# Attention scores laid out head by head, block transposes of the probabilities on VectorE, softmax shift and residual on GpSimd

## The reference

```python
# per sequence; z = layernorm of x + a projection of attention-pooled block sums
qkv = z @ W_attn + b_attn                       # heads: H = 32, D = 8, S = 32 tokens
scores = einsum('bhqd,bhkd->bhqk', q, k) / sqrt(8)
scores = where(causal, scores, -10000) + alibi  # cols <= rows
probs = softmax(scores, axis=-1)
x = x + (einsum('bhqk,bhkd->bhqd', probs, v) merged) @ W_proj + b_proj
hs = GRU(cond, x)                               # 32 dependent steps
x = x + hs @ (weight * scale).T + bias
```

## Time and profile before

| | |
|---|---|
| median of three runs | 445.61 us |
| the profiled execution | 445.15 us, of which the span is 443.3 us |
| attention stage, with the start | the first 257 us of the span |
| GRU stage | the rest |
| PE busy, whole span | 423.8 us, 96% |
| DVE, ACT, POOL busy | 326.1, 236.4, 93.2 us |

### The profile page before, as it was taken

One profiled execution on the slowest core, in us unless ns is written; L12 is line 12 of the kernel. 1 busy time (PEld: TensorE's weight loads), 2 busy tenths in 40 slices (PEclk: granted clock), 3 DMA queues, 4 the chain that ended last, 5 costly groups with the idle time before them and its releaser, 6 DMA issues.

```text
span 443.3 us, 13432 instructions
## 1 busy us (share of the span) xinstructions
PE 423.8 (96%) x5448; PEld 350.9 (79%) x5448; DVE 326.1 (74%) x995; ACT 236.4 (53%) x553; POOL 93.2 (21%) x114
## 2 busy tenths in 40 slices
PE   8899999999999999999999899999999999999994
PEld 5656687786877878778687698899999999999984
DVE  3587888798888877879777844677776677777665
ACT  7355657566575675755666753444444444444341
POOL 7663142432132221322235500000000000000000
PEclk9999999999999999999999999999999999999999
DMA  7942413223133141231213000001000000000001
GB/s 289 394 183 70 135 40 100 70 61 109 35 90 96 50 120 39 86 95 53 74 33 92 27 1 2 0 2 47 20 31 24 25 24 26 25 24 25 24 25 71
DMA packets 34268, 30.36 MB, mean 68 GB/s; under 512 B 4128, under 2 KB 29344, under 8 KB 34208
## 3 DMA queue, kind: packets, MB, share of 16 engines
q1 hardware_dynamic: 34208, 29.51, 20.5%
HBM read 16.92 MB, written 8.39 MB: 57 GB/s over the span
## 4 chain that ended last, share of the span: by engine, by line
PE 75%; DVE 15%; ACT 4%; issue 3%; POOL 1%; DVEq 0%; ACTq 0%; POOLq 0%
PE ps_a L1267 10%; PE ps_s L1432 7%; PE ps_t L1432 6%; PE ps_o L1432 6%; PE ps_s L1327 6%; PE ps_s L1488 5%; PE ps_t L1488 5%; PE ps_a L1488 4%; PE ps_t L1340 4%; PE ps_m L1371 4%; PE ps_m L1488 4%; PE ps_o L1351 3%; PE ps_m L1363 3%; DVE mx L963 2%; ACT y L599 2%
## 5 line engine op out<-in xcount | busy, mean ns | idle before, releaser
L531 POOL TENSOR_TENSOR sc<-masked,mx 128x512 f32<-128x512 f32 x32 | 45.7, 1429 | 143.3 <-DVE mx L963 143.3
L955 DVE COPY_PREDICATED masked<-kst,ps_s 128x512 f32<-128x512 int32 x64 | 44.1, 736 | 6.1 <-PE ps_s L1327 5.8
L1267 PE MATMUL ps_a<-yT_r,w_qkv_r 128*128 128x512 f32 x180 | 46.0, 403 | 1.3 <-DVE yT_r L936 0.9
L754 ACT ACTIVATE zg<-ps_t,brz 128x128 f32<-128x128 f32 x64 | 20.1, 365 | 39.6 <-PE ps_t L1432 37.3
L963 DVE TENSOR_REDUCE mx<-masked 128x16 f32<-128x512 f32 x64 | 40.5, 674 | 0.0
L1267 PEld LDWEIGHTS ps_a<-yT_r,w_qkv_r 128*128 128x128 f32 x180 | 32.6, 188 | 9.6 <-issue 2.8
L637 ACT ACTIVATE sc<-sc 128x512 f32<-128x512 f32 x64 | 37.3, 621 | 4.2 <-DVE sc L969 2.9
L1101 DVE SCALAR_TENSOR_TENSOR rg<-ps_o,vec,rg 128x128 f32<-128x128 f32 x64 | 19.5, 346 | 24.8 <-PE ps_o L1432 23.8
L570 ACT ACTIVATE pT<-ps_t 128x512 f32<-128x512 f32 x64 | 34.9, 595 | 4.5 <-PE ps_t L1340 3.4
L1327 PE MATMUL ps_s<-kbd,qn 64*32 64x256 f32 x1024 | 36.3, 382 | 0.8 <-issue 0.8
L1432 PEld LDWEIGHTS ps_s<-hT,w_hh 128*128 128x128 f32 x256 | 33.1, 191 | 4.9 <-DVE hT L1119 2.8
(11 more groups left out here) (159 smaller groups left out, 827.2 us busy)
## 6 DMA issues: line engine op xcount, KB each, us to landing
xf<-in_x_feat SPq DMA_DIRECT2D x8, 512.0 KB, 9.5
xg<-in_x_tok SPq DMA_DIRECT2D x8, 512.0 KB, 5.1
kbd<-kn SPq DMA_DIRECT2D x128, 32.0 KB, 1.9
v_dram<-vn SPq DMA_DIRECT2D x16, 256.0 KB, 2.5
vbd<-v_dram SPq DMA_DIRECT2D x64, 64.0 KB, 2.1
out_feat<-ost SPq DMA_DIRECT2D x16, 256.0 KB, 2.0
w_qkv<-in_wqkv SPq DMA_DIRECT2D x1, 768.0 KB, 9.7
w_ih<-in_wih SPq DMA_DIRECT2D x1, 768.0 KB, 13.3
```

Of the source, the lines that this page charges most:

```text
L531: nc.gpsimd.tensor_tensor(shifted, kept, m.unsqueeze(2).to_broadcast([P, NH // 2, S]), ALU.subtract).then_inc(sc_sub[1], 1)
L754: nc.scalar.activation(dst[:, c, :], gate_part(gate, c, t), ACT.Sigmoid, bias=brz[:, b0 + c:b0 + c + 1]).then_inc(done, 1)
L955: nc.vector.copy_predicated(kept, keep.unsqueeze(1).to_broadcast([P, NH // 2, S]), ps_s[:, h * 512:(h + 1) * 512].rearrange("p (h k) -> p ...
L1267: last = nc.tensor.matmul(bank, w_qkv_r[a][:, c, first_col + m * P:first_col + (m + 1) * P], yT_r[b][:, c, :], start=(a == b == c == 0), s ...
```

## The change

The scores now use tiles of 32 rows by 32 columns of TensorE. Each product contracts 32 rows and covers four heads' keys of one sequence (128 columns instead of 256), so a tile has 32 products instead of 16. The output's partitions are (head of four, query), and its columns are (head quad, sequence, quad member, key). Since every 32x32 block of the probabilities is then one head and sequence, it can be turned where it stands: two DVE block transposes (`nc.vector.transpose`, 512 columns each) go straight from `sc` to `pT`, in place of eight PE transposes and two ACT copies. The freed PSUM `ps_t` takes the queries' and values' projections, `ps_a` keeps the keys'. `kbd` is double-buffered at the same total size, with 4 DMAs instead of 8 per half, and the loads no longer wait for the scores of the running group. Both halves of the softmax shift are done by POOL, and so is the residual of all tiles but the last, behind an ACT copy `xo` for each. The order of the lists changes: ACT computes the exponentials of tile n at the start of step n, around `attn_out(n-1)`, and makes `xo` directly behind them; DVE does `rest_of_y` before the mask, and `transpose_probs(n)` before `softmax_max(n+1)` and `token_stats`; POOL puts `inverse_std` ahead of `residual`.

```diff
-RH = 2
-KH = P // RH // 8
+KH = NQ // C                      # 4
-BY_POOL = range(NT - GT, NT - 1)
+BY_POOL = range(NT - 1)
-            kbd = ... nc.sbuf_tensor("kbd", [P, C, KH, GC], F32)
+            kbd = ... nc.sbuf_tensor("kbd", [P, 2, C, KH, GC], F32)
-            pT = ... nc.sbuf_tensor("pT", [P, NQ, P], F32)
+            pT = ... nc.sbuf_tensor("pT", [P, NH * S], F32)
+        def value_bank(k, h):
+            return (ps_m[:, :], ps_a[:, 0:512])[h] if k == 0 else ps_t[:, h * 512:(h + 1) * 512]
...  (sync)
-                for h in range(KH):
-                    sp.dma_start(kbd[h:P:KH, :, h, cols], kn[h:P:KH, :, cols]).then_inc(k_in[half], DMA)
+                for j in range(KH):
+                    sp.dma_start(kbd[j:P:KH, k % 2, :, j, cols], kn[j:P:KH, :, cols]).then_inc(k_in[half], DMA)
                 sp.wait_ge(k_out, 2 * g + 4)
-                sp.wait_ge(sc_mm, 8 * g + 4)
+                if g > 0:
+                    sp.wait_ge(sc_mm, GT * g)
                 load_k(g + 1, 0)
-                sp.wait_ge(sc_mm, 8 * g + 8)
                 load_k(g + 1, 1)
...  (gpsimd)
-                _, kept, shifted, m = halves(n % 2)[1]
-                pool.wait_ge(sc_max, 2 * n + 2)
-                nc.gpsimd.tensor_tensor(shifted, kept, m..., ALU.subtract).then_inc(sc_sub[1], 1)
+                for h, kept, shifted, m in halves(n % 2):
+                    pool.wait_ge(sc_max, 2 * n + h + 1)
+                    nc.gpsimd.tensor_tensor(shifted, kept, m..., ALU.subtract).then_inc(sc_sub, 1)
                     if n + 1 < NT:
                         softmax_shift(n + 1)
+                    if i == 2 and g + 2 < NG:
+                        inverse_std(g + 2)
                     if n - 1 in BY_POOL:
                         residual(n - 1, (n - 1) // GT, (n - 1) % GT)
                     if i == 1 and g + EARLY < NG:
                         block_sums(g + EARLY)
-                    if i == 2 and g + 2 < NG:
-                        inverse_std(g + 2)
...  (scalar)
-            def softmax_exp(n, p):            # and probs_out(n), both removed
+            def softmax_exp(n, p, h):
+                act.wait_ge(sc_sub, 2 * n + h + 1)
+                part = sc[:, p, h * 512:(h + 1) * 512]
+                nc.scalar.activation(part, part, ACT.Exp).then_inc(sc_exp, 1)
             act.wait_ge(w_ready, 1)
             q_chunk(0, 0)
+            round_proj(1, proj_ps_1)          # was ahead of q_chunk(0, 0)
             def tile_step(g, i):
+                softmax_exp(n, n % 2, 0)
                 if i == 0 and not last_group:
                     round_y(g + 1, 0)
                     round_y(g + 1, 1)
                 if n > 0:
                     attn_out(n - 1)
-                probs_out(n)
+                softmax_exp(n, n % 2, 1)
+                if n - 1 in BY_POOL:
+                    projection_out(n - 1)
...
-                if n - 1 in BY_POOL:
-                    projection_out(n - 1)
-                if n + 1 < NT:
-                    softmax_exp(n + 1, (n + 1) % 2)
...  (vector)
                 for h, kept, _, _ in halves(p):
                     if not first:
-                        dve.wait_ge(sc_sub[h], n)
-                    dve.wait_ge(sc_mm, 2 * n + h + 1)
+                        dve.wait_ge(sc_sub, 2 * n + h - 1)
+                    dve.wait_ge(sc_mm, n + 1)
-            def softmax_shift(n, p):          # removed from DVE
+            def transpose_probs(n, p):
+                dve.wait_ge(pv_mm, n)
+                for h in range(2):
+                    cols = slice(h * 512, (h + 1) * 512)
+                    dve.wait_ge(sc_exp, 2 * n + h + 1)
+                    nc.vector.transpose(pT[:, cols], sc[:, p, cols]).then_inc(pt_out, 1)
+                if i == 0 and g + 1 < NG:
+                    rest_of_y(g + 1)
                 if n + 1 < NT:
                     softmax_mask(n + 1, (n + 1) % 2)
-                if i == 0 and g + 1 < NG:
-                    rest_of_y(g + 1)
                 if norm_ahead and i == 2:
                     add_proj(g + 2, ps_a)
+                transpose_probs(n, n % 2)
+                if n + 1 < NT:
+                    softmax_max(n + 1, (n + 1) % 2)
                 if norm_ahead and i == 2:
                     token_stats(g + 2)
-                if n + 1 < NT:
-                    softmax_max(n + 1, (n + 1) % 2)
-                    softmax_shift(n + 1, (n + 1) % 2)
                 if norm_ahead and i == 2:
                     mean_and_variance(g + 2)
                 if n > 0 and n - 1 not in BY_POOL:
                     residual(n - 1, (n - 1) // GT, (n - 1) % GT)
...  (tensor)
+            def score_column(q, b):
+                return q // KH * 512 + (b * KH + q % KH) * S
-                for c in range(C):
-                    for r in range(RH):
-                        rows = slice(r * P // RH, (r + 1) * P // RH)
-                        for b in range(TB):
-                            out_cols = slice((r * C + c) * KH * S, (r * C + c + 1) * KH * S)
-                            ... matmul(ps_s[b * S:(b + 1) * S, out_cols], qn[rows, g % 2, c, cols],
-                                       kbd[rows, c, :, cols], tile_position=(r * P // RH, b * S))
+                for b in range(TB):
+                    for c in range(C):
+                        out_col = score_column(c * KH, b)
+                        for r in range(HG):
+                            rows, head = slice(r * S, (r + 1) * S), (r + c) % HG
+                            ... matmul(ps_s[head * S:(head + 1) * S, out_col:out_col + KH * S],
+                                       qn[rows, g % 2, c, cols], kbd[rows, g % 2, c, :, cols],
+                                       tile_position=(r * S, head * S))
-            def transpose_probs(n, p, first=False):   # removed from PE, with its call
                 if n - 1 in BY_POOL:
-                    pe.wait_ge(xo_out, C * (n - BY_POOL[0]))
+                    pe.wait_ge(xo_out, C * n)
                 elif i == 1:
-                    pe.wait_ge(k_out, 2 * k + h + 1)
+                    if k > 0:
+                        pe.wait_ge(v_out, 2 * k)
                 elif i == 2:
-                    pe.wait_ge(q_out, 2 * k + h + 1)
-                    if 0 < k < NG - 1:
-                        pe.wait_ge(z_done, 2 * k + 2 + h + 1)
+                    if k > 0:
+                        pe.wait_ge(q_out, C * k + h + 1)
```

More of the change, by code:

```diff
@@ L400, in _ @@
             load_k(0, 1)
+            sp.wait_ge(v_out, 1)
+            save_v(0, 0)
             sp.wait_ge(v_out, 2)
-            save_v(0, 0)
             save_v(0, 1)
@@ L629, in v_half @@
                 nc.scalar.activation(vn[:, half, :, :].rearrange("p h (t w) -> p t h w", t=TH),
[L630 removed]
+                                     value_bank(k, half).rearrange("p (t h w) -> p t h w", t=TH, h=HG),
                                      ACT.Identity, scale=key_factor).then_inc(v_out, 1)
[L633 to L644 removed]
+            def softmax_exp(n, p, h):
+                act.wait_ge(sc_sub, 2 * n + h + 1)
+                part = sc[:, p, h * 512:(h + 1) * 512]
+                nc.scalar.activation(part, part, ACT.Exp).then_inc(sc_exp, 1)
             def projection_out(n):
@@ L1028, in _ @@
             cond_mean(2)
-            add_proj(1, ps_t)
+            add_proj(1, ps_a)
             token_stats(1)
@@ L1066, in tile_step @@
                     cond_scores(3)
+                if i == 0 and g in (0, 2):
+                    cond_shift(2 + g // 2)
+                transpose_probs(n, n % 2)
                 if i == 1 and g in (0, 2):
@@ L1260, in project_qk @@
             def project_qk(k, first_col, done, m):
-                bank = ps_a[:, m * GC:(m + 1) * GC]
+                bank = (ps_a if done is k_mm else ps_t)[:, m * GC:(m + 1) * GC]
                 for a, b in ((0, 0), (1, 0), (0, 1)):
@@ L1320, in scores, with prob_block @@
                     pe.wait_ge(sc_out, 2 * n)
-                for c in range(C):
-                    for r in range(RH):
-                        rows = slice(r * P // RH, (r + 1) * P // RH)
-                        for b in range(TB):
-                            cols = slice(i * P + b * S, i * P + (b + 1) * S)
-                            out_cols = slice((r * C + c) * KH * S, (r * C + c + 1) * KH * S)
-                            last = nc.tensor.matmul(ps_s[b * S:(b + 1) * S, out_cols], qn[rows, g % 2, c, cols],
-                                                    kbd[rows, c, :, cols], start=True, stop=True,
-                                                    tile_position=(r * P // RH, b * S))
-                        if c == C - 1:
-                            last.then_inc(sc_mm, 1)
-            def transpose_probs(n, p, first=False):
-                for h in range(2):
-                    pe.wait_ge(sc_exp, 2 * n + h + 1)
-                    if not first:
-                        pe.wait_ge(pt_out, 2 * n - 1 + h)
```

(21 more changed lines are left out.)

61 lines of the change are left out of this document (21 added, 40 removed).

## The result

| | kernel before | kernel after |
|---|---|---|
| median of 4 runs each, us | 445.65 (443.76 to 445.76) | 453.36 (452.29 to 454.61) |
| profiled execution, us | 445.15, span 443.3 | 452.29, span 450.5 |
| ratio, 95% interval | | 1.0184 [1.0141, 1.0227] |

A ratio leaves out executions more than 1.5% above the fastest of their kernel, which here concerns four of the ten of e1_fill alone.

What follows compares the result with a forecast made beforehand. PE looked busy, but its transposes filled a wait for ACT; POOL's shift enters both rings. Group 0 -0.06, groups 1 to 5 +3.8, group 6 -0.64 and +0.66, last +1.32 and +2.25: 445.15 + 7.3 = 452.5 us, range 439 to 463.

Steps and rivals of the forecast that it cites:

- What bounds PE: PE's transposes, 28 us over 32 tiles, fill the wait for ACT's oT; removing them saves only 0.13 us a step.
- The steps i = 0, 1 and 2: Groups 1 to 5: i = 0 0.38 us less, i = 1 0.13 less, PE finishing i = 2 at 6.67.
- Rival E: PE is the bound and all 28 us of its transposes come off: 417 us; chance 0.05.
- Block transposes, 1.18 us a pair: Two DVE block transposes of 512 columns take 1.18 us a tile, like neighbouring DVE operations at 0.59 each.
- Rival C: A DVE block transpose takes 1.18 us instead of 0.59, adding 11.8 us: 464.3 us; chance 0.12.
- Scores, 1.02 us: A tile's scores on PE keep their 1.02 us, with twice as many products of half the columns.
- Rival D: Row tiles take turns at a PSUM bank, scores 3.5 us instead of 1.02: 510 us; chance 0.03.
- y comes later, +1.27 us a group: Steps i = 2 and 3 together take 14.6 us, not 13.33: xo waits for POOL's residual, and y queues behind xo.
- POOL's shift: Both softmax shift halves on POOL cost 2.86 us a tile instead of 1.43, entering both rings.
- The ring round: Last five steps: single-buffered mask waits for POOL's shift of the previous tile, 5.5 us a round, binding without projections.
- steps 28 and 29: In the last group, these go from 4.84 to 5.5 us each, bound by POOL's ring: +1.32 in all.
- the tail: Steps 30 and 31 go from 8.2 us to 5.5 + 4.95, the last without a mask: +2.25.

Runs made afterwards that it cites:

- e1_fill: Kernel after, with the first half of the projections ahead issued before the output projection on PE; ratio 0.9986 of the kernel before, median of ten 446.07 us.
- e4: Kernel before, leaving out six of the eight PE transposes of the probabilities of each tile; 442.74 us, ratio 0.9942.
- e3: Kernel after, with the first half of the softmax shift back on DVE and the second half alone on POOL; 458.26 us, ratio 1.0291.
- e5: Kernel after, with 24 tiny PE products added ahead of the output projection in most steps with projections ahead; 459.32 us, ratio 1.0319.
- e9: Kernel after, with 32 products of 2 columns added at the start to move the code behind them; 469.4 us, ratio 1.0564.
- e12: e11 with 32 products of 2 columns added at the start; 467.55 us, ratio 1.0496.
- e2: Kernel after, with the normalisation of tokens y put before the copies xo on ACT at i = 3; 452.64 us, ratio 1.0169.
- e6: Kernel after, with e1_fill's and e2's moves, plus DVE statistics before transposes and POOL inverse_std before shift at i = 2; 447.36 us, ratio 1.0062.
- e11: Kernel after, with e1_fill's and e2's moves and the second half of the values' projection moved from i = 2 to i = 3; 449.73 us, ratio 1.0106.
- e7: e6 with scores behind the projection's first half at i = 1 and 2, and DVE's mask behind its transposes there; 454.57 us, ratio 1.0221.
- e8: Kernel after, leaving out the score products of two of the four sequences from tile 2 on; 442.72 us, ratio 0.9957.
- e10: Kernel before, with 32 products of 2 columns added at the start to move the code behind them; 457.97 us, ratio 1.0283.

## Why the prediction was right, and where it wasn't

- **What bounds PE.** Right. PE's 28 us of transposes were not to be had, since they stood in the wait for `oT`: 18.3 us of that wait appeared, and e4 shows it in the kernel before (21 us of work out, 2.6 us gained). The steps i = 0, 1 and 2 came within 0.1 us of their forecast when undisturbed. Rival E was wrong.
- **Block transposes, 1.18 us a pair.** 1.28 measured (1.27 to 1.30), not 0.59 each but 0.64. Rival C is out. The estimate of 1.24 us for 512 columns, worked out from a bf16 figure of the Trainium skill's "VectorE: DVE Perf Modes", The three transpose paths, was about double of that.
- **Scores, 1.02 us.** The 64 instructions take 1.08 to 1.12 us on the chain, their loads 0.88. Rival D is out. Its 3.5 us has no working; from eight abreast to two would be 4 x 1.02 = 4.1. Four row tiles write different partitions of one bank here and the time is within 0.1 us of that of before, so the Trainium skill's "TensorEngine Tiling (Array Packing)", Gotcha 1: PSUM Pressure, taken literally, doesn't hold for this case.
- **y comes later, +1.27 us a group.** Right in sign and chain: DVE's transposes ahead of the maxima, `on` at 8.65 (forecast 8.47), then `oT`, projection, `xo`, y. Wrong in one link: `xo` didn't wait for POOL's residual (ready at 157.78) but for the projection (159.83), because POOL's shifts took 2.06 us and not 2.86. Even undisturbed the projection would have let `xo` go only at 157.9, 0.1 us behind that residual. Undisturbed, the pair i = 2 and 3 is 14.1, not 14.6: 2.4 us less in five groups.
- **The mis-sized term: POOL's shift.** 1.43 us was read from a row in which DVE ran beside it. Alone it is 1.03 to 1.06 (e3 has both). The ring round is then 5.5 - 0.8 = 4.7 us; measured 4.73, against 4.8 to 4.9 before. So steps 28 and 29 gained 0.2 us instead of losing 1.3, and the tail lost 0.6, not 2.3. The chain of waits doesn't run through POOL there. One turn of the last group, from scores to scores:
```profile
250.59 1.12 PE ps_s L1327 x64
...
252.47 0.10 DVE masked L948
...
253.10 1.30 DVE pT L964 x2
...
254.53 0.84 PE ps_o L1345 x61
255.38 1.12 PE ps_s L1327 x64
```
  Scores, mask, transposes, `probs_v`, scores: 4.8 us through DVE and PE. POOL's shift that would hold the next second mask ends at 257.09, and that mask starts at about 257.25. The two rings are nearly equal once the shift is at its true price, so that POOL's ring binds was wrong, or at best a tie. The 1.0 us that PE waits there in each step for DVE's second transpose is one of the waits that the weight loads' row calls "issue".
- **Missed: PE's gaps and the clock.** About 3.4 us in i = 2 and 3 of groups 2 to 4, and part of what i = 0 and 1 lack. This and the next point made up for the 3.2 us that steps 28 to 31 did not lose and the 2.4 of the chain to y; 452.5 against 453.36 is closer than the steps were, by luck.
- **Missed: +1.4 us at the first scores**, where the second half of the values' projection now stands behind scores(0) on PE.

Shown: the `oT` wait (e1, e4); POOL's price (e3); gaps that lie elsewhere when unchanged code is moved (e5, e9, e12); and that they need the dense stretch. The nine kernels in which a tile's 64 score instructions follow `probs_v` directly (the kernel after, e1, e2, e3, e5, e6, e9, e11, e12) each have a stall of 1.6 us or more inside the scores, wherever their code lies; with the two set apart at i = 1 and 2 (e7) the longest is 0.5 us, and with 32 instructions (the kernel before, e4, e8, e10) none reaches 1.0 us. That the stalls wait for instructions is shown as far as timing can: all 47 end at the same distance behind a packet of the instruction queue. Why that block is late where it is stays open; of the 36 such packets between the first and last scores of the kernel after only four have a stall inside the scores behind them. Not shown either: that a kernel stalls in the same places in each execution, since each was profiled once; and what brings the clock down, since equal gaps were followed by 0.50 in one place and 1.00 in another.

## What to carry to other kernels

Before you take work off the busiest engine, look at what that work covers: if a round trip to another engine lies behind it, put other independent work there in the same edit (e1_fill gave back 9 us with one moved call). Read an instruction's price from a row with the same neighbours as it will have, since moving the neighbour away changes it. When idle time is put down to "issue", see first whether something that the instruction reads was finished just before it. If not, and if it grows with the number of small products, compare two positions of the same code, by several executions each, before you trust a reordering of 1%.

## What the runs showed of the hardware that I had not expected

- POOL's 128x512 subtraction: 1059 ns without DVE's subtraction beside it, 1430 ns with it.
- With 128 small PE instructions and as many weight loads in some 1.9 us, the weight loads stalled for up to 1.9 us inside the scores in the kernel after and 2.9 us in e5, at places that differ with position; each such stall ended 1.2 to 1.6 us behind a 16 KB packet of the instruction queue. "issue" idle of the weight loads from 44 to 257 us: 19.4 us before, 21.9 with half the score products, 27.5 after, 43.3 in e11.
- Behind 1.8 us without work the granted clock was 0.50 for about 3 us, and a projection took 2.07 us instead of 1.16; in e2 twelve key products at 0.50 took 4.53 instead of 3.05. Behind a gap of 1.9 us at 124.93 it stayed at 1.00.
- Products of 2 columns with 128x128 weights at the start of the kernel: 64 instructions in 13.81 us, 0.22 us each, though each streams two columns.
